# A constant matmul ahead of each wait for the scores, in the last layer of a four-layer graph network

## The reference, cut to what matters

```
h = (x @ W).reshape(N, 4, 128)
e = leaky_relu(a_src[src] + a_dst[dst], 0.2)      # one score per edge and head
m = segment_max(e, dst)
w = exp(e - m[dst])
z = segment_sum(w, dst)
out = segment_sum(h[src] * (w / z[dst]), dst).mean(heads) + bias
```

## Time and profile before

| | |
|---|---|
| median of three runs | 5179.06 us |
| the profiled execution | 5169.83 us |
| its span, first to last instruction | 5168.5 us |
| mean granted TensorE clock of the span | 0.698 of full speed |
| edge loop of the last layer, slots | 3740 to 5077 us |
| gathers of the last layer end | about 5047 us |

### The profile page before, as it was taken

How to read it: one execution, slowest core, us unless ns; L and a number is a source line. 1 busy time by engine, 2 the same in 40 slices (tenths; PEclk the granted TensorE clock), 3 DMA queues, 4 the chain that set the end, 5 groups by cost and what they waited for, 6 DMA issues and landing times. The chain is left out here.

```text
span 5168.5 us, 65297 instructions
## 1 busy us (share of the span) xinstructions
PE 2696.1 (52%) x13348; PEld 2262.6 (44%) x13348; DVE 2622.3 (51%) x7266; ACT 1809.7 (35%) x4202; POOL 2979.9 (58%) x3172
## 2 busy tenths in 40 slices
PE   2555556543655555555333333334555555565557
PEld 2444445443444444455233333334444444444446
DVE  4433434433555555556333333334567766667677
ACT  2433333311333333322111111113455555555556
POOL 3666666666666666665566666666455555555552
PEclk8776667666777777667665656556777766667779
DMA  5333333322333333321322222233551111111111
GB/s 120 101 102 95 102 97 108 98 59 56 101 102 101 93 102 93 93 65 50 100 85 89 89 89 85 90 89 101 98 97 41 41 40 40 39 39 40 42 41 29
DMA packets 242878, 405.96 MB, mean 79 GB/s; under 512 B 68322, under 2 KB 141691, under 8 KB 242492
## 3 DMA queue, kind: packets, MB, share of 16 engines
q0 software_dynamic: 99456, 206.27, 15.5%
q10 hardware_dynamic: 69920, 120.96, 8.3%
q1 hardware_dynamic: 73116, 74.56, 5.1%
HBM read 331.90 MB, written 67.79 MB: 77 GB/s over the span
## 5 line engine op out<-in xcount | busy, mean ns | idle before, releaser
L742 POOL DMA_INDIRECT t_work<-d_T,t_tabG x3100 | 2926.7, 944 | 2069.7 <-SPq L833 1003.9
L1636 PE MATMUL ps<-t_work,t_acc 128*128 x2592 | 490.8, 347 | 413.1 <-issue 292.6
L1636 PEld LDWEIGHTS ps<-t_work,t_acc 128*128 128x128 f32 x2592 | 441.2, 254 | 478.7 <-issue 478.0
L1709 DVE TENSOR_TENSOR t_acc<-t_acc,ps 128x128 f32 (+1 forms) x732 | 209.8, 287 | 730.9 <-remote 575.3
L2124 PE MATMUL ps<-t_work,t_hT 128*128 x1960 | 419.4, 379 | 300.4 <-ACT t_hT L2112 143.6
L2124 PEld LDWEIGHTS ps<-t_work,t_hT 128*128 128x128 f32 x1960 | 359.9, 275 | 372.8 <-issue 372.8
L1698 DVE TENSOR_TENSOR t_hT<-t_work,ps 128x512 f32<-128x512 f32 x244 | 167.0, 685 | 633.6 <-issue 360.2
L627 ACT ACTIVATE t_acc<-ps,t_bcol 128x1024 f32<-128x1024 f32 x98 | 109.1, 1113 | 1053.4 <-DVE ps L640 761.7
L1811 ACT COPY ps<-t_acc 128x512 f32 x244 | 140.5, 588 | 934.6 <-issue 610.4
L1636 PE MATMUL ps<-t_hT,t_acc 128*128 128x128 f32 x1296 | 266.6, 390 | 379.1 <-DVE t_acc L1709 286.1
L1636 PEld LDWEIGHTS ps<-t_hT,t_acc 128*128 128x128 f32 x1296 | 251.8, 298 | 395.6 <-DVE t_hT L1698 223.1
(11 more groups left out here) (205 smaller groups left out, 4451.2 us busy)
## 6 DMA issues: line engine op xcount, KB each, us to landing
d_edge_net<-t_acc ACTq DMA_DIRECT2D x98, 512.0 KB
t_acc<-d_edge_net SPq DMA_DIRECT2D x98, 512.0 KB
t_work<-d_T,t_tabG POOLq DMA_INDIRECT x3100
t_acc<-in_edge_attrT ACTq DMA_DIRECT2D x96, 512.0 KB
t_acc<-d_T SPq DMA_DIRECT2D x1792, 0.5 KB
t_acc<-d_T SPq DMA_DIRECT2D x896, 0.5 KB
t_work<-d_T SPq DMA_DIRECT2D x896, 0.5 KB
t_acc<-d_T ACTq DMA_DIRECT2D x12, 790.1 KB
```

What stands on the lines that cost most here:

```text
L742: pool.indirect_dma_start(out=work[:, at:at + width], out_offset=None, in_=table, in_offset=bass.IndirectOffsetOnAxis(ap=idx[:, g * QUAD + ...
L1636: last = pe.matmul(sums(layer, s, width), masks[s % MASKS][:, k, :], rows_k, start=(k == 0), stop=(k == QUAD - 1))
L1709: dve.tensor_tensor(out=o, in0=o, in1=sums(layer, s, width), op=ALU.add).then_inc(e_acc[layer], 1)
```

## The change

`turn_scores(n)` waits first for the bank to be free (`s_lk`), then multiplies the identity with 256 constant columns into the first half of that bank, and only then waits for the scores (`s_tw`) and turns them. The product is never read: the transposes write over it. Nothing else is changed.

```diff
         def turn_scores(n):
 
+            passed_by(pe, s_lk, n - 1)
+            pe.matmul(ps[:, PT + n % 2, 0:2 * P], ident, cst[:, 0:2 * P], start=True, stop=True)
             pe.wait_ge(s_tw, n + 1)
-            passed_by(pe, s_lk, n - 1)
             for k in range(QUAD):
                 last = pe.transpose(ps[:, PT + n % 2, k * P:(k + 1) * P], tw[n % 2][:, k * P:(k + 1) * P], ident)
             last.then_inc(s_pt, 1)
```

## The result

The change makes the kernel slower. Its median is 5206.07 us over 20 runs (5182.99 to 5222.49), that of the kernel before 5175.61 us over 20 runs (5167.03 to 5196.99). The ratio is 1.0056, with a 95% interval from 1.0048 to 1.0065: 30 us more, and the whole interval lies beyond the 0.2% that can be told. The forecast was 5193 us, in a range from 5158 to 5225.

A forecast was written before the change was run, and what follows sets the result against it. It took VectorE to bound warm turns, TensorE cold ones and no engine the standing ones. 22 us passed on less 8 us given back made 14 us, moving 5179 to 5193 us; range 5158 to 5225.

The forecast's parts named there:

- cold turns: Turns of the last layer's edge loop at half TensorE clock, 4.04 us each, TensorE the bound; 88 of 231 assumed.
- the stands: Stretches of the last layer's edge loop where TensorE starts nothing, 4.66 us in the one shown; no engine sets them.
- The cost of the matmul: Before the scores on TensorE, one added 256-column matmul takes 0.45 us at full clock, 0.9 us at half.
- What is hidden: Before the scores, in 143 of 231 turns the matmul runs in TensorE's idle time; nothing is charged for these.
- The 22 us passed on by 88 cold turns: Next sums start 0.8 us late; 0.5 us survives the following turn, halved to 0.25 us for each of 88 turns.
- The 8 us given back by the clock: Cold turns made warm by added TensorE work return 0.37 us each, 33 us in all 88; a quarter was taken.
- the clock rival: The added matmul holds TensorE's clock in the edge loop, at 0.8 or above; kernel faster, some 5155 us; chance 0.24.
- The rule on transposes: On TensorE, transposes don't count as busy for the clock as matmuls do; it would give all 33 us back, about 5146.
- The stands, held fixed: The length of the edge loop's stands was taken as unchanged, having no known cause; a change would make the prediction wrong.
- That all is swallowed: Something other than TensorE sets the stands, so a push under 1 us vanishes in them; 5174 to 5188 us; chance 0.20.
- Payment in full: Every late sum delays GpSimd's next group and the next stand; up to 70 us, more likely some 50; chance 0.14.

## Why the prediction was right, and where not

The direction came out and the time lies in the range: 5193 us forecast, 5206 measured, a loss of 30 us for one of 14. The way to the number was luck. The forecast put the loss in the cold turns and held the stands fixed; in the profiles the turns outside the stands lose nothing, and all of the loop's loss is in the stands.

**The cost of the matmul** was right. It has 490 matmul instructions, two for each, and as many loadings of weights. At half clock the pair takes 0.85 us (0.9 forecast), at full clock 0.44 (0.45), and the moved wait shows no cost of its own where it was tried alone, without stands.

**What is hidden** was right in kind. The idle time before the scores fell to 147.8 us (some 150 forecast). But the turns without any were to stay near 90 of 231, and are 228 - 115 = 113 of 228: in some, the matmul used up a short break.

**The 22 us passed on by 88 cold turns** is the step that failed. The push is there, 0.6 us at the next sums in the turn shown (0.8 forecast). I let 0.5 us survive the next turn and halved it. In the rows the next turn, whose clock was already rising, regained it all. Cold turns were to grow from 4.04 to about 4.3 us. Of all turns under 6.5 us, those with a mean granted clock under 0.55 went from 62 to 25, and from 4.24 to 4.18 us each. So the 88 turns without a wait were not all cold either. All turns under 6.5 us together became 3 us shorter, where the forecast had them 14 us longer.

**The 8 us given back by the clock** were too small: I gave back a quarter of the cold turns, with a loop clock of 0.71 to 0.76 as the sign. It came to 0.78, between that and the 0.80 at which the clock rival would have been right, and more than half of the cold turns are gone. I had argued that in a cold turn more work can't raise the clock. The turns shown don't contradict that: the cold one is still at 0.50. But the turn behind it climbs earlier, with its sums at 1.52 us in place of 2.09. At 0.37 us a turn the 37 turns that are no longer cold would be worth 14 us, of which 3 us show in the sum of these turns; whether the push took the rest is not shown. The rule on transposes in the Trainium skill ("TensorE: Matmul & The Clock Gate", Part 4), by which the added matmul would weigh more than a quarter, leads in the direction in which I erred; no run here tells it from a plain count of columns.

**The stands, held fixed**, are what made the loss. The prediction said that it would be wrong if their length changed, since it had no cause for them. They did change: 8.30 to 8.85 us each, 30 us in all. TensorE's idle time in them grew from 424 to 447 us, 23 of these 30, so it is for the most part not the added work itself that fills them. The stand also meets TensorE at another place: its longest idle time lies before the sums in 58 of 85 such turns, where it was 48 of 87, and before the scores in the others. That is the move of idle time in the groups by line. Three causes remain for the added length: the 0.45 to 0.9 us of work, by way of later sums and later freed groups; the number of instructions and semaphore steps; or the earlier arrival that the higher clock brings. The last can't carry it alone: if the stands end where they did, an earlier arrival adds to them only what the other turns lost, 3 us. No run tells the first two apart, and with one profiled execution on each side part of the 26.5 us can be spread: the median difference of 30 us is firm, its place in the loop rests on that one pair.

**The rivals.** That the clock is held got its mechanism in part and its time not at all: where GpSimd's gathers set the pace it is worth nothing, 1.0003 at 0.98 in place of 0.90. That all is swallowed is what happens where there are no stands. Payment in full did not come to its 50 to 70 us, and where there are no stands four matmuls cost nothing. But its path, late sums that free a group late and so hold up the next gather and the next stand, is the one on which the loss shows: GpSimd's waits for freed groups grew by 26.4 us (398.1 to 424.5). No run where the stands are tested it, so it stays open.

No kernel tried is faster than the one before.

## What to carry to other kernels

Work put into an engine's idle time is free as long as another engine is the bound, and a matmul that lifts TensorE's clock then earns nothing either: one, two and four matmuls in the same place measure that room directly. The bound need not be the engine with the most busy time: here VectorE is busy for 862 of 900 us and GpSimd for 679, but a fixed gap of 0.30 us behind each gather leaves GpSimd no room at all. Count starts, not busy time. When a loop has standing turns whose cause the trace doesn't name, don't hold them fixed in an estimate: put them into the range as a term of either sign; here it was 30 us over some 86 stands, 0.35 us for each. And before a change is kept or dropped for half a per cent, compare it on more than one chip: this one costs 0.56% where the result was measured and nothing that can be told where it was measured again.

## What the hardware showed that was not expected

The same program took 5176 us where the result was measured, and 4123 to 4128 us on three chips in the experiments. Whether the chip itself makes the difference is not shown. The clock doesn't explain it. A warm turn lasts 3.67 us in the slower one, and with the waits swapped 97 of the 244 turns on a faster one lie between 3.6 and 3.7 us.

What differs in the loop is the 87 standing turns: it takes 1364.5 us there and 965.5 here. That is 399 of the 1042 us between these two profiles; the other 643 arise in the layers ahead of it (the first link starts at 3705.7 and at 3062.9 us). The gathers tell it for the whole program. By the pages, GpSimd's 3100 gathers have 2069.7 us of idle time before them in the slower one and 1037.9 us in the faster, so nearly all of the difference is time for which a gather was held up.

The stands look like late releases and not like work. In the one in the turn from 4053.32 no engine starts an instruction from 4054.70 to 4057.15 us; then Sync, VectorE, GpSimd and ScalarE all do within 0.1 us. Sync shows the same thing by itself. These are its transfers of L791 and the register instructions beside them, duration as least/median/longest in ns. First the kernel before at 5170 us, then the kernel with the waits swapped at 4128 us:

```profile
L791 SPq DMA_DIRECT2D t_work<-d_T x883: 5/228/1433, 3740.0 to 4984.5; - x177
L791 SPq MOVE t_work<-d_T x882: 4/29/1432, 3740.3 to 4984.5; - x177
```

```profile
L791 SPq DMA_DIRECT2D t_work<-d_T x875: 227/228/486, 3099.9 to 3966.3; - x175
L791 SPq MOVE t_work<-d_T x874: 29/29/29, 3100.2 to 3966.2; - x175
```

A move of a register, which waits for no semaphore and no data, took 29 ns each of 874 times in the faster one, and up to 1432 ns in the slower. In the kernel before, the stands come every two or three turns (74 of the 86 gaps between them), on all engines together, and end with the gathers. What holds the engines there stays open.
